# A four-block kernel: eight of 32 value projections computed in an earlier seam, kept in DRAM and read back

## What is computed

```python
x = x + _L0_xattn_ref(_layernorm(x), ctx, ...)      # first attention
x = x + _L0_ffn_ref(_layernorm(x), ...)             # first mixture of experts (MoE)
x = x + _L1_xattn_ref(_layernorm(x), ctx, ...)      # image attention, 16 heads of 16
x = x + _L1_ffn_ref(_layernorm(x), ...)             # 4-bit feed-forward
x = x + _L2_xattn_ref(_layernorm(x), ctx, Wq, Wk, Wv, Wo)   # second full attention
x = x + _L2_ffn_ref(_layernorm(x), ...)             # LoRA layer
x = x + _L3_xattn_ref(_layernorm(x), ctx, mask)     # memory readout
x = x + _L3_ffn_ref(_layernorm(x), ...)             # grouped attention, then a second MoE
```

```python
q = (inputs_q @ Wq).reshape(b, sq, 16, 128) / sqrt(128)
k = (inputs_kv @ Wk).reshape(b, skv, 16, 128)
v = (inputs_kv @ Wv).reshape(b, skv, 16, 128)      # inputs_kv is ctx
attn = softmax(einsum('bqhd,bkhd->bhqk', q, k))
ctx_out = einsum('bhqk,bkhd->bqhd', attn, v).reshape(b, sq, 2048)
return ctx_out @ Wo
```

## Time and profile before

| | us |
|---|---|
| Three runs | 1204.44, 1205.94, 1203.35 (median 1204.44) |
| The profiled execution | 1198.61 |
| its span | 1196.8 |

### The profile page before, as it was taken

How to read it: one execution, slowest core, us unless ns; L and a number is a source line. 1 busy time by engine, 2 the same in 40 slices (tenths; PEclk the granted TensorE clock), 3 DMA queues, 4 the chain that set the end, 5 groups by cost and what they waited for, 6 DMA issues and landing times.

```text
span 1196.8 us, 19996 instructions
## 1 busy us (share of the span) xinstructions
PE 1049.0 (88%) x6826; PEld 797.5 (67%) x6826; DVE 709.2 (59%) x1684; ACT 510.2 (43%) x1785; POOL 320.1 (27%) x440
## 2 busy tenths in 40 slices
PE   6898888599999868889999999999789999995693
PEld 3665555499999745667878777786556666664472
DVE  5577785711222267887556556567667777775544
ACT  2255557133333146775433333333546655553120
POOL 6253332112332234553000000002122212220572
PEclk9999999589999959999999999999999999998797
DMA  6764442789889406201211110022000000000795
GB/s 190 268 212 144 147 145 81 257 317 323 322 328 332 141 28 221 62 1 30 56 36 36 36 36 11 26 88 89 1 1 5 5 5 5 5 5 13 236 308 180
DMA packets 85216, 141.71 MB, mean 118 GB/s; under 512 B 10089, under 2 KB 58489, under 8 KB 79201
## 3 DMA queue, kind: packets, MB, share of 16 engines
q1 hardware_dynamic: 71193, 116.84, 29.7%
q0 software_dynamic: 4416, 12.06, 3.0%
q10 hardware_dynamic: 9508, 11.55, 2.9%
HBM read 117.51 MB, written 22.72 MB: 117 GB/s over the span
## 4 chain that ended last, share of the span: by engine, by line
PE 62%; DVE 11%; DMA 8%; issue 6%; ACT 5%; SPq 4%; POOL 3%; DVEq 0%; POOLq 0%; ACTq 0%
PE P L968 7%; PE P L978 7%; PE P L1925 4%; PE P L1965 4%; PE P L2111 4%; PE P L2058 4%; DMA scr_qk<-big 3%; PE P L1916 3%; PE P L2064 2%; PE P L2877 2%; PE P L2100 2%; PE P L2086 2%; PE P L1937 2%; SPq L329 2%; DMA big<-placed 1%
## 5 line engine op out<-in xcount | busy, mean ns | idle before, releaser
L139 POOL TENSOR_TENSOR lrs<-lve,mhalf 128x1 f32<-128x1 f32 x64 | 36.4, 569 | 316.9 <-DVE lve L130 285.7
L576 DVE TENSOR_REDUCE small<-P 128x2 f32<-128x512 f32 x128 | 84.2, 683 | 40.3 <-PE P L403 40.2
L1009 ACT ACTIVATE big<-P,big 128x128 f32<-128x128 f32 x184 | 52.6, 369 | 124.3 <-PE P L968 124.3
L2252 ACT ACTIVATE big<-P,small 128x128 f32<-128x128 f32 x128 | 45.3, 366 | 128.4 <-DVE small L2435 128.4
L656 ACT ACTIVATE big<-P 128x512 f32<-128x512 f32 x128 | 73.6, 599 | 54.0 <-PE P L423 46.6
L968 PE MATMUL P<-big 128*128 128x128 f32 x736 | 88.1, 279 | 0.0
L968 PEld LDWEIGHTS P<-big 128*128 128x128 f32 x736 | 86.3, 196 | 0.1
L1111 DVE COPY big<-P 128x256 f32<-128x256 f32 x23 | 9.8, 425 | 124.8 <-PE P L978 124.8
L978 PE MATMUL P<-big 128*128 128x256 f32 x368 | 83.1, 379 | 0.0
L978 PEld LDWEIGHTS P<-big 128*128 128x128 f32 x368 | 68.2, 190 | 8.4
L271 PE MATMUL P<-CT,big 128*128 128x256 f32 (+1 forms) x224 | 68.1, 433 | 6.1 <-ACT big L248 4.3
(11 more groups left out here) (386 smaller groups left out, 2513.8 us busy)
## 6 DMA issues: line engine op xcount, KB each, us to landing
big<-b_w SPq DMA_DIRECT2D x23, 1028.0 KB
big<-b_w SPq DMA_DIRECT2D x23, 1024.0 KB
big<-scr_qk SPq DMA_DIRECT2D x96, 96.0 KB
big<-keys_t SPq DMA_DIRECT2D x8, 1024.0 KB, 6.0
big<-i_wgu SPq DMA_DIRECT2D x23, 352.0 KB
keys_t<-XNT ACTq DMA_DIRECT2D x24, 256.0 KB, 2.1
big<-moe_y SPq DMA_DIRECT2D x16, 256.0 KB, 4.3
big<-i_wd SPq DMA_DIRECT2D x23, 176.0 KB
```

The costliest lines, as they stand in the source:

```text
L576: dve.tensor_reduce(negM[:, h, :], P[:, h % 2, :].rearrange("p (c s) -> p c s", c=2), AX.X, ALU.max, negate=True).then_inc(a_max, 1)
L1009: act.activation(hT[j % 2][:, f, :], P[:, 2 * (j % 2) + f // 4, f % 4 * 128:f % 4 * 128 + 128], ACT.Gelu_apprx_tanh, bias=w1x[j % 3][:, 2 ...
```

## The change

The values of group 2 of every batch row, 8 of the 32 (`EARLY(m)` is m % 4 == 2), are no longer projected in their steps. A part of Wv (512 KB, columns 1024 to 1535) is loaded into a free piece of the buffer at the end of the MoE's transfers. PE makes the eight projections in the seam: four behind `project_context(1)`, one each at the end of windows -4 and -3, and two at the end of window -2. ACT copies each out of PSUM banks 2 and 3 and issues its transfer (256 KB) to the DRAM tensor `VALS`; the first `scores` wait until all eight are copied. In the attention, steps without a projection skip it on PE and on DVE, `value_row` on SP reads the row's values into `e_V[0]` in their place once the values of group 0 have been used, and `weigh4` of the group waits for that transfer. SP loads three parts of Wv instead of four. The semaphores' counts are moved accordingly (`made4`, `FT0`, `MT0` and others).

```diff
@@ s1_sp
+            sp.dma_start(v_w, e_wv.rearrange("(k p) n -> p k n", p=128)[:, :, 1024:1536]).then_inc(v_ld, 16)
             sp.wait_ge(b_sc, 16 * NB)
@@
+        EARLY_AT = {-4: (4,), -3: (5,), -2: (6, 7)}
@@ s23_pe
+            def early_values(i):
+                if i == 0:
+                    pe.wait_ge(v_ld, VLD0 + 16)
+                if i >= 2:
+                    pe.wait_ge(v_ev, i - 1)
+                for k in range(KD):
+                    t = pe.matmul(P[:, 2 + i % 2, :], CT[:, k, i * T:i * T + T], v_w[:, k, :], start=(k == 0),
+                                  stop=(k == KD - 1))
+                t.then_inc(v_pe, 1)
@@ scores
+                if h == 0:
+                    pe.wait_ge(v_ev, B)
@@
             project_context(1)
+            for i in range(4):
+                early_values(i)
             turn_routed(0)
@@
                 if 1 <= w + 5 < B:
                     turn_routed(w + 5)
+                for i in EARLY_AT.get(w, ()):
+                    early_values(i)
@@ s23_act
+            def early_values(i):
+                act.wait_ge(v_pe, i + 1)
+                act.activation(v_out[i], P[:, 2 + i % 2, :], ACT.Copy).then_inc(v_ev, 1)
+                act.wait_ge(v_ev, i + 1)
+                act.dma_start(VALS[i], v_out[i]).then_inc(v_st, 16)
+
+            for i in range(4):
+                early_values(i)
             act.wait_ge(d_st, D_READY)
             copy_routed(0)
@@
                 if 1 <= w + 5 < B:
                     copy_routed(w + 5)
+                for i in EARLY_AT.get(w, ()):
+                    early_values(i)
@@
+        def value_row(sp, b):
+            sp.wait_ge(e_pv, 4 * b + 1)
+            sp.dma_start(e_V[0], VALS[b]).then_inc(v_rd, 16)
@@ s4_sp
+            sp.wait_ge(v_st, 16 * B)
@@
-            for g in range(4):
+            for g in (0, 1, 3):
@@ s57_sp
+            value_row(sp, 0)
             key_row(sp, 2)
@@
             for b in range(3, B):
+                value_row(sp, b - 2)
                 key_row(sp, b)
+            value_row(sp, B - 2)
@@
             for g in range(4):
+                if g == 3:
+                    value_row(sp, B - 1)
@@ values4
+                if EARLY(m):
+                    return
@@ weigh4
-                pe.wait_ge(e_vs, m + 1)
+                if EARLY(m):
+                    pe.wait_ge(v_rd, VRD0 + 16 * (m // 4) + 16)
+                else:
+                    pe.wait_ge(e_vs, made4(m))
```

More of the change, by code:

```diff
@@ L1823, in build @@
         CLEAR = 6
-        ld_x2, FLD0 = f_ld, 16
+        ld_x2, FLD0 = f_ld, 32
+        v_ld, VLD0 = f_ld, 16
+        v_pe, MT0 = m_T, B
+        v_ev, FT0 = f_T, B
+        v_st = c_PTv
         ld_c2, MLD0 = m_ld, 16
@@ L1827, in build, with EARLY, made4 @@
         k_w, CLD0, ELD0, HLD0, HLD20 = [c_ld, e_ld, h_ld, h_ld2], 32, 16, 16, 16
-        k_ct, ILD0 = i_ld, 16
+        k_ct, ILD0 = i_ld, 16 + 16 * B
+        v_rd, VRD0 = i_ld, 16
+        v_w = big1[:, 14360:15384].rearrange("p (k n) -> p k n", k=KD)
+        v_out = [big1[:, 6168 + 512 * i:6680 + 512 * i] for i in range(B)]
+        VALS = nc.dram_tensor("values_g2", (B, 128, 512), F32, kind="Internal").ap()
+        def EARLY(m):
+            return m % 4 == 2
+        def made4(m):
+            return m + 1 - (m + 2) // 4
         k_pe, EY0 = e_y, KP
@@ L1899, in s57_sp @@
             for g in range(4):
+                if g == 3:
+                    value_row(sp, B - 1)
                 sp.wait_ge(e_qk, NM - 3 + g)
                 sp.dma_start(h_wqs[:, g], wq[:, :, 512 * g:512 * g + 512]).then_inc(h_ld if g < 2 else h_ld2, 16)
-            sp.wait_ge(e_v, NM - 2)
+            sp.wait_ge(e_v, made4(NM - 3))
             sp.dma_start(h_wos[:, 8:16], wo[:, 8:16]).then_inc(h_ld3, 16)
@@ L1920, in values4 @@
             def values4(m):
+                if EARLY(m):
+                    return
                 b, g = divmod(m, 4)
                 if m > 0:
-                    pe.wait_ge(e_vs, m)
+                    pe.wait_ge(e_vs, made4(m - 1))
                 for k in range(KD):
@@ L2019, in third @@
                     b = row_at(G, 7)
-                    pe.wait_ge(f_T, b + 1)
+                    pe.wait_ge(f_T, FT0 + b + 1)
                     pe.matmul(P[:, 6, 0:D], f_xaT, f_lbs, start=True, stop=True).then_inc(f_y, 1)
@@ L2030, in third @@
                     b = row_at(G, 10)
-                    pe.wait_ge(m_T, b + 1)
+                    pe.wait_ge(m_T, MT0 + b + 1)
                     pe.matmul(P[:, 6, 0:D], m_pt, CX[:, b, :], start=True, stop=True).then_inc(m_y, 1)
@@ L2123, in turn_fed @@
                     t.then_inc(tb_pe, 1)
-            pe.wait_ge(e_ld, ELD0 + 144)
+            pe.wait_ge(e_ld, ELD0 + 128)
             pe.wait_ge(tb_ev, TURNED[B - 1])
@@ L2183, in s47_pe @@
                     if m == 0:
-                        pe.wait_ge(e_vs, NM)
+                        pe.wait_ge(e_vs, made4(LAST))
                     scores(m + 1)
@@ L2422, in copy_values4 @@
             def copy_values4(m):
-                dve.wait_ge(e_v, m + 1)
+                if EARLY(m):
+                    return
+                dve.wait_ge(e_v, made4(m))
                 if m >= 2:
@@ L2820, in weights2 @@
                              i_wd[bass.ds(e, 1)].rearrange("a p n -> p (a n)")).then_inc(i_w[j % NW], 16)
+            sp.wait_ge(v_rd, VRD0 + 16 * B)
             sp.dma_start(i_gs, i_gate.rearrange("(k p) e -> p k e", p=128)).then_inc(i_ld, 16)
```

## The result

Six runs of the changed kernel have a median of 1198.64 us against 1204.51 us of the kernel before, 5.9 us less. The ratio of the runs is 0.9945, 95% interval 0.9924 to 0.9967, so 6.6 us faster (4.0 to 9.2). A second set on another occasion (experiment 8) gave 0.9941, 0.9923 to 0.9959. The forecast was 7.8 us less than before.

A forecast was written before the change was run, and what follows sets the result against it. PE was taken to bound the kernel almost everywhere, the seam being a chain with PE waits. 11.8 us gained in the attention and 4.0 lost in the seam take the median from 1204.44 to 1196.6 us; range 1191.0 to 1204.0.

The forecast's parts named there:

- Steps 9 to 29: Attention, six steps without a projection: the LoRA product starts right behind ACT's row copy, 1.26 us gained each, 7.6 together.
- part 1: The attention without eight value projections: 7.6 + 1.2 + 3.0 = 11.8 us gained.
- Step 1: Attention: `up3` could start 1.72 us earlier but waits for DVE's L1635; 1.2 us gained.
- Step 5: Attention: DVE's masks start without the values' copy ahead of them, so PE's later wait ends sooner; 3.0 us gained.
- The seam: Between expert loop and row 2's bias: projections 0 to 4 fill PE's waits, 5 to 7 lengthen the path; 4.0 us lost.
- a third between the ends: Seam cost chosen between 0.4 us gained (2.4 GHz throughout) and 12.9 us lost (1.2 GHz): 4.0 us lost.
- the two waits I named: Seam: PE idles about 2.3 us before the turned query and some 2 us behind the first scores; one may drop the clock.
- ACT's issue: Seam: issuing one early transfer on ACT takes 0.34 us, the median of one group; another group showed 0.99 us.
- the writes delay the gather: Rival, seam: ACT's writes to DRAM take from the gather's transfer rate, 1.4 us, total 1198.0 us; chance 0.07.
- The clock holds all through: Rival: PE's clock stays up throughout the seam, which then costs -0.4 us; kernel 1192.2 us; chance 0.12.
- the seam eats all: Rival: projections 5 to 7 run at 1.2 GHz and ACT's issues take 0.99 us; kernel 1207.5 us, slower; chance 0.10.
- The attention gains less: Rival: ACT's or DVE's chain ends each row, so the attention gains only 4.2 us; 1204.2 us, no change; chance 0.07.

The follow-up runs named there:

- experiment 8: The changed kernel, unaltered, measured again beside the earlier placement on one chip; ratio to the kernel before 0.9941, median 1196.47 us.
- experiment 7: The kernel before with one move: in step 5 DVE prepares the masks ahead of its copy of the values; ratio to before 0.9995.
- experiment 3: The changed kernel with early projections 5, 6 and 7 each placed one window earlier; ratio to the kernel before 0.9911.
- experiment 6: The changed kernel with only projections 0 to 3 made in the seam and all 32 made in the attention; ratio to the kernel before 0.9986.
- experiment 5: The changed kernel's eight early projections and copies without transfers to DRAM, all 32 projections again in the attention; ratio to the kernel before 1.0002.
- experiment 2: The changed kernel without early projections or transfers out; the attention skips group 2's projections and reads a weight instead; ratio to the kernel before 0.9899.
- experiment 4: The changed kernel with projections 5 and 6 one window earlier and 7 behind the first scores; ratio to the kernel before 0.991.
- experiment 9: The changed kernel with projections 5, 6 and 7 one window earlier, measured again beside the changed kernel; ratio to before 0.9929, median 1193.75 us.

## Why the prediction was right

**The sum.** Predicted -11.8 + 4.0 = -7.8 us; measured -11.1 by the traces for the attention, +3.4 for the seam in the first profile, and -6.6 and -7.1 over the runs. The time of 1198.64 us lies 2.0 us above the forecast of 1196.6 and inside its range. The forecast for the profiled execution, 1190.8 us, missed by 8.0: 3.8 us of it lie ahead of every added instruction and 3.8 in the entry, two stretches that vary between executions and for which the prediction had no term.

**Steps 9 to 29.** Each was to gain 1.26 us by PE's starting 0.05 us behind ACT's copy. They gained 1.13, 1.15, 1.15, 1.14, 1.25 and 1.14. The mechanism is as stated, and so is the handover: in step 17 ACT's copy ends at 706.44 and the product starts at 706.49. But from a wait the product takes 1.42 us to the start of the next operation (706.49 to 707.91), where before it took 1.31 (706.92 to 708.23). Over six rows that is 0.6 us of the 0.7 by which part 1 was too large.

**Step 1** gained 1.1 us (1.2 forecast), by DVE's L1635 as named. **Step 5** gained 3.0 (3.0 forecast); experiment 7 shows apart that the masks' place was what PE waited for.

**The seam.** That projections 0 to 3 are free, 4 free in its wait, and 5 to 7 on the path was right, and experiments 3 and 6 show it by moving or removing them. The choice of a third between the ends (4.0 us) was right by luck as much as by reason: the clock fell at the two waits I named, for 3.4 and 6.8 us in two profiles and for 3.4 and 3.4 in the other two, and the distance to the bias grew by 3.44, 4.04, 2.35 and 2.70 us in the four profiles with all eight projections at the change's places. Up to the attention's first projection it grew by 3.4, 5.0, 5.1 and 5.5, since the clock fell again later in three of them. So the seam's mean price is nearer 4.8 us, which with -11.1 gives -6.3.

**ACT's issue** was taken at 0.34 us and took 0.33; why the other row's issues (0.99, at 40.8 to 49.2 us) are slower no run tests. The Trainium skill, DMA: Bandwidth & Descriptors, "Issuing engines are not separate DMA queues", states that transfers share the same 16 engines, whichever engine issued them. The trace agrees: in the microsecond from 424 the writes and the gather together bring the share to 1.07, at 387 GB/s. The rival that the writes delay the gather, with 1.4 us, fails all the same: experiment 5 puts what transfers and issues cost the path at 0.24 us. Of DVE's additions of gathered rows only the first waits for the gather, and the first turned row starts 10.43 us after the contexts' projections, 10.53 before.

**The rivals.** "The clock holds all through" and "the seam eats all" both failed on the clock's taking a middle course. "The attention gains less" fell with experiment 2.

**A sign of being wrong that came.** The expert loop was to end by 413.5; the contexts' projections behind it ended at 417.29 (413.67 + 3.62), against 413.49 before. As a sign it was ill chosen: the 3.8 us had built up ahead of the added load.

**What I did not see** is that the placement left most of the seam's price on the table: the rows that I read held a wait of 4.22 us, room for two projections at 2.4 GHz, of which the change uses one. Nor did I follow ACT's early copies through its squares and POOL's root to DVE, the chain on which experiment 4 ends.

## What to carry to other kernels

Work moved from a stage bound by TensorE into a seam is free only inside a wait and only up to its length: cover each wait with as many whole pieces as fit, and put none ahead of an instruction that another engine is waiting for. A second chain may be as long, here ACT's squares, POOL's root and DVE's norm: beyond that point a piece taken off TensorE's path brings nothing, and the copies that the moved work needs on another engine have to be placed as carefully as the work. A single pair of profiles can hide the result: compare distances between equal operations, and see which of them also vary between executions of the same instructions.

## What was not expected of the hardware

The granted clock of a stretch in which PE is partly busy is a matter of the single execution. In the entry of the grouped attention, eleven profiles with the same PE instructions there show 0 to 12.9 us at 1.2 GHz and distances from 35.82 to 40.17 us. Filling the start of a seam does not keep the clock up for the rest: in experiment 6 it fell 5 us after the filled wait had ended, within the next wait of 4.18 us, and it came back only 17 us later, although a kernel with more work in the same seam had it back after 3.4 us. A low stretch of 3.4 us also appeared there behind the seam at 457.6 and before the attention at 546.3, with PE busy all through both; it had been busy 1.47 of the 4.0 us before the first and 1.52 of the 3.4 us before the second. The kernel before, the first profile of the changed kernel and experiments 2, 3, 7 and 9 have neither stretch.
